# Two sets of constant factors in a graph network kernel: both loaded ahead, constant rows counted in pairs of sets

## What is computed

```python
def layer(h, params):
    W, b, g, beta = params
    h = h * norm_out
    agg = jax.ops.segment_sum(h[src], dst, num_segments=n)
    agg = agg * norm_in
    out = agg @ W + b
    out = _layer_norm(out, g, beta)
    out = jax.nn.gelu(out, approximate=False)
    return (out, None)
h, _ = jax.lax.scan(layer, features, (Ws, bs, ln_g, ln_b))
x = _layernorm(x + h)
```

## Time and profile before

| | |
|---|---|
| median of 3 runs | 1358.86 (1360.18, 1358.86, 1354.14) |
| the profiled execution | 1357.35, its span 1355.7 |
| granted clock, mean of the span | 0.835 |
| busy, share of the span | TensorE 70%, DVE 62%, POOL 56%, ACT 35% |

### The profile page before, as it was taken

How to read it: one execution, slowest core, us unless ns; L and a number is a source line. 1 busy time by engine, 2 the same in 40 slices (tenths; PEclk the granted TensorE clock), 3 DMA queues, 4 the chain that set the end, 5 groups by cost and what they waited for, 6 DMA issues and landing times.

```text
span 1355.7 us, 27832 instructions
## 1 busy us (share of the span) xinstructions
PE 944.8 (70%) x5568; PEld 729.4 (54%) x5568; DVE 841.6 (62%) x1938; ACT 475.7 (35%) x779; POOL 764.9 (56%) x921
## 2 busy tenths in 40 slices
PE   7899857733896978787796898689847889940000
PEld 7675213303785757576674776577736777730000
DVE  9787788835475565747456367346814446757786
ACT  4431232012433333343333433343334433323455
POOL 3477208520565555555654655556536746648885
PEclk9889866755997979899898899699959999975555
DMA  7932499021626354452633632652256679557998
GB/s 273 377 98 60 126 340 383 4 79 36 169 81 202 118 180 125 142 186 106 197 121 131 210 114 97 217 177 87 93 199 191 199 191 396 207 180 252 318 314 300
DMA packets 118241, 246.59 MB, mean 182 GB/s; under 512 B 20271, under 2 KB 21119, under 8 KB 118171
## 3 DMA queue, kind: packets, MB, share of 16 engines
q1 hardware_dynamic: 73868, 133.26, 27.7%
q0 software_dynamic: 31680, 89.43, 22.9%
q10 hardware_dynamic: 12624, 23.14, 4.6%
HBM read 130.14 MB, written 115.64 MB: 181 GB/s over the span
## 4 chain that ended last, share of the span: by engine, by line
PE 37%; DMA 18%; issue 14%; DVE 11%; POOL 11%; DVEq 4%; ACT 3%; ACTq 1%; POOLq 1%; SPq 0%
PE ps_y L1870 6%; DMA rows<-h_rows,slot 6%; PE ps_y L1865 5%; PE ps_y L1866 5%; PE ps_a L1836 5%; DMA h_rows<-rows 5%; POOL rows L752 4%; POOL rows L826 4%; PE ps_y L1710 3%; DMA rows<-h_rows,idx 3%; DVEq L443 2%; DMA constant_factors<-row_factors 2%; PE ps_a L1690 2%; PE ps_z L1729 2%; DVE agg_t L943 1%
## 5 line engine op out<-in xcount | busy, mean ns | idle before, releaser
L1836 PE MATMUL ps_a<-sel,rows 128*128 128x128 f32 x2080 | 302.6, 299 | 93.8 <-DVE sel L1203 53.2
L1836 PEld LDWEIGHTS ps_a<-sel,rows 128*128 128x128 f32 x2080 | 272.0, 207 | 128.5 <-issue 126.8
L1203 DVE TENSOR_SCALAR sel<-iota,by_tile 128x128 f32<-128x128 f32 x307 | 125.2, 411 | 253.0 <-issue 225.4
L752 POOL DMA_INDIRECT rows<-h_rows,slot x230 | 220.1, 957 | 109.6 <-issue 78.6
L1557 ACT ACTIVATE agg_t<-ps_a 128x508 f32 x260 | 155.0, 596 | 216.3 <-PE ps_a L1836 173.8
L777 POOL TENSOR_TENSOR s_lo<-agg_t,s_hi 128x512 fp32r<-128x512 f32 x122 | 157.3, 1292 | 108.5 <-ACT s_hi L1562 108.0
L1865 PE MATMUL ps_y<-w_all,s_hi 128*128 128x512 f32 x488 | 191.6, 393 | 3.5 <-ACT s_hi L1562 2.5
L1866 PE MATMUL ps_y<-w_all,s_hi 128*128 128x512 f32 x488 | 190.2, 390 | 0.0
L1870 PE MATMUL ps_y<-w_all,s_lo 128*128 128x512 f32 x488 | 131.2, 391 | 1.9 <-POOL s_lo L777 1.9
L1358 DVE BATCH_NORM_STATS2 small<-ps_y 128x6 f32<-128x512 f32 x122 | 85.1, 697 | 43.4 <-PE ps_y L1870 43.2
L1562 ACT ACTIVATE s_hi<-agg_t 128x512 fp32r (+1 forms) x122 | 75.9, 628 | 90.7 <-PE ps_y L1870 48.0
(11 more groups left out here) (318 smaller groups left out, 1503.7 us busy)
## 6 DMA issues: line engine op xcount, KB each, us to landing
h_rows<-agg_t SPq DMA_DIRECT2D x2, 22528.0 KB, 67.9
h_rows<-rows SPq DMA_DIRECT2D x92, 256.0 KB, 2.0
h_rows<-rows ACTq DMA_DIRECT2D x87, 256.0 KB, 3.7
out<-agg_t SPq DMA_DIRECT2D x78, 256.0 KB, 4.3
agg_t<-in_x SPq DMA_DIRECT2D x19, 1024.0 KB, 13.5
rows<-in_Ws SPq DMA_DIRECT2D x32, 256.0 KB, 2.7
w_raw<-in_Ws SPq DMA_DIRECT2D x28, 256.0 KB, 4.3
rows<-h_rows,slot POOLq DMA_INDIRECT x230, 3.7
```

Source lines behind the costliest of these rows:

```text
L752: g.indirect_dma_start(out=rows[:, k, :], out_offset=None, in_=table[:, :], in_offset=bass.IndirectOffsetOnAxis(ap=slot[:, k:k + 1], axis=0))\
L1203: return v.tensor_scalar(sel[:, k % GS, :], iota[:, :], rel[:, bass.ds(i, 1)], wgt[:, bass.ds(i, 1)], ALU.is_equal, ALU.mult)
L1836: m = mm(ps_a[k % GS][:, b, :], rows[:, k, b * P:(b + 1) * P], sel[:, k % GS, :], start=True, stop=True)
```

## The change

Factors and vectors get two sets: set 0 on partitions 0 to 9, set 1 on partitions 32 to 41 of the same tiles, each with its own semaphore. Both are loaded at the start of the product stage. The rows of a layer are counted in **duos** of two trios (768 rows, rounded up, at least one); every turn of a loop makes one trio from each set. POOL's loop runs over all duos, and each turn loads both sets for the next one, in the last turn too, where the factors are loaded and not used; the factor table gets 768 more rows in front, so that such a load stays inside it. DVE waits, before its third selection, for all loads of both sets to have landed, in place of the last matmul. The constants `landed` and the semaphore targets follow. Not shown: the table's fills in SP's part (longer by 768 rows), the new counts in POOL's arithmetic (`DUO * P` for `TRIO * P`), and the renamed arguments.

```diff
-ITS_MIN, PAIRS_MIN, TRIOS_MIN = 1, 3, 2
+DUO = 2 * TRIO
+AHEAD_ROWS = DUO * P
+ITS_MIN, PAIRS_MIN, DUOS_MIN = 1, 3, 1
...
-    coef_d = nc.dram_tensor("row_factors", (KINDS, LC, SLACK + PADDED), f32).ap()
+    coef_d = nc.dram_tensor("row_factors", (KINDS, LC, AHEAD_ROWS + SLACK + PADDED), f32).ap()
...
-        co_out, co_vec, co_fac = rows[:, 6:9, :], co_vec_t[0:2 * KINDS, :], co_fac_t[0:2 * KINDS, :, :]
+        co_out = rows[:, 6:9, :]
+        co_vec = [co_vec_t[h * 32:h * 32 + 2 * KINDS, :] for h in range(2)]
+        co_fac = [co_fac_t[h * 32:h * 32 + 2 * KINDS, :, :] for h in range(2)]
...
-        co_in = sem("constant_factors_in")
+        co_in = [sem(f"constant_factors_in{h}") for h in range(2)]
...
-            trios = within(word >> 16, 0, N // (TRIO * P) + 1 - TRIOS_MIN) + TRIOS_MIN if L > 0 else 0
+            duos = within(word >> 16, 0, N // (DUO * P) + 1 - DUOS_MIN) + DUOS_MIN if L > 0 else 0
...
+        def factor_row(rb, g):
+
+            return within(rb - (g + 1) * (TRIO * P) + AHEAD_ROWS, 0, AHEAD_ROWS + SLACK + PADDED - TRIO * P)
...
-            def load_factors(L, n):
+            def load_factors(L, n, h):
 
-                own = coef_d[:, L - 1, bass.ds(trio_row(rb, n), TRIO * P)]
-                g.dma_start(co_fac.rearrange("r a n -> r (a n)"), both(own)).then_inc(co_in, 16)
+                own = coef_d[:, L - 1, bass.ds(factor_row(rb, n * 2 + h), TRIO * P)]
+                g.dma_start(co_fac[h].rearrange("r a n -> r (a n)"), both(own)).then_inc(co_in[h], 16)
...
-                    with pool.Fori(1, constants[0]) as n:
-                        pool.wait_ge(co_pe, (constants[1] + n) * TRIO)
-                        pool.sem_inc(tick, 1)
-                        load_factors(L, n)
+                    with pool.Fori(0, constants[0]) as n:
+                        for h in range(2):
+                            pool.wait_ge(co_pe, (constants[1] + n) * DUO + (h + 1) * TRIO)
+                            pool.sem_inc(tick, 1)
+                            load_factors(L, n + 1, h)
                     stored(pb * 2)
-                    landed = constants[0] + constants[1]
+                    landed = (constants[0] + constants[1]) * 2
...
-                    g.dma_start(co_vec, vec_d[L + 1, :, :].bitcast(f32r)).then_inc(co_in, 16)
-                    load_factors(L + 1, 0)
+                    for h in range(2):
+                        g.dma_start(co_vec[h], vec_d[L + 1, :, :].bitcast(f32r)).then_inc(co_in[h], 16)
+                        load_factors(L + 1, 0, h)
                 w_stage(pairs, pb)
...
-                    trios, cb = constants
-                    dve.wait_ge(co_pe, (cb + trios) * TRIO)
-                    dve.sem_inc(dve_tick, 1)
+                    duos, cb = constants
+                    for h in range(2):
+                        dve.wait_ge(co_in[h], (cb + duos) * 16 + L * 32)
+                        dve.sem_inc(dve_tick, 1)
                 select(tile + AHEAD - 1, AHEAD - 1).then_inc(sel_ok, 1)
...
-                with act.Fori(0, trios) as g:
-                    constant_trio(L, cb + g, g)
+                with act.Fori(0, duos) as g:
+                    for h in range(2):
+                        constant_trio(L, (cb + g) * 2 + h, g * 2 + h)
...
-                with pe.Fori(0, trios) as g:
-                    pe.wait_ge(co_in, (cb + g) * 16 + (L + 1) * 16)
-                    pe.sem_inc(pe_tick, 1)
-                    for k in range(TRIO):
-                        pe.wait_ge(co_h, done((cb + g) * TRIO - TRIO + k + 1))
-                        pe.sem_inc(pe_tick, 1)
-                        mm(ps_co[k], co_fac[:, k, :], co_vec, start=True, stop=True).then_inc(co_pe, 1)
+                with pe.Fori(0, duos) as g:
+                    for h in range(2):
+                        n = (cb + g) * DUO + h * TRIO
+                        pe.wait_ge(co_in[h], (cb + g) * 16 + L * 32)
+                        pe.sem_inc(pe_tick, 1)
+                        for k in range(TRIO):
+                            pe.wait_ge(co_h, done(n - TRIO + k + 1))
+                            pe.sem_inc(pe_tick, 1)
+                            mm(ps_co[k], co_fac[h][:, k, :], co_vec[h], start=True, stop=True).then_inc(co_pe, 1)
```

More of the change, by code:

```diff
@@ L427, in layer_counts @@
             its = within((word >> 8) & 255, 0, NE // UN - ITS_MIN) + ITS_MIN
-            trios = within(word >> 16, 0, N // (TRIO * P) + 1 - TRIOS_MIN) + TRIOS_MIN if L > 0 else 0
+            duos = within(word >> 16, 0, N // (DUO * P) + 1 - DUOS_MIN) + DUOS_MIN if L > 0 else 0
             if earlier is None:
-                return pairs, its, trios, 0, 0, 0
-            return (pairs, its, trios) + tuple(earlier[n] + earlier[n + 3] for n in range(3))
+                return pairs, its, duos, 0, 0, 0
+            return (pairs, its, duos) + tuple(earlier[n] + earlier[n + 3] for n in range(3))
         def place(eng, n, most):
@@ L524, in _ @@
                 sp.wait_ge(made_ok, 2)
-                sp.dma_start(coef_d[n:n + 2, :, SLACK:].rearrange("k l (p n) -> p (k l) n", n=NR),
+                sp.dma_start(coef_d[n:n + 2, :, AHEAD_ROWS + SLACK:].rearrange("k l (p n) -> p (k l) n", n=NR),
                              halves.bitcast(f32).rearrange("p k l n -> p (k l) n")).then_inc(fac_st, 16)
@@ L707, in _ @@
             link(g.memset(num_f[:, 2, 0:1], 0.0))
-            for n, size, extra in ((0, 2 * P, 1), (1, UN * ET, 0), (2, TRIO * P, 0)):
+            for n, size, extra in ((0, 2 * P, 1), (1, UN * ET, 0), (2, DUO * P, 0)):
                 scaled(num_f[:, n, :], num_f[:, n, :], extra * size - (size - 1) / 2 + (1 - extra) * (size - 1), size)
             whole(num_f)
-            for n, least in enumerate((PAIRS_MIN, ITS_MIN, TRIOS_MIN)):
+            for n, least in enumerate((PAIRS_MIN, ITS_MIN, DUOS_MIN)):
                 link(g.tensor_scalar(num_f[:, n, :], num_f[:, n, :], float(least), float(-least), ALU.max, ALU.add))
@@ L806, in _ @@
             for L in range(LAYERS):
-                pairs, its, trios, pb, ib, cb = counts
-                sum_stage(L, hbufs[(L - 1) % 2] if L > 0 else x, its, ib, pb, (trios, cb))
+                pairs, its, duos, pb, ib, cb = counts
+                sum_stage(L, hbufs[(L - 1) % 2] if L > 0 else x, its, ib, pb, (duos, cb))
                 if L + 1 < LAYERS:
@@ L1340, in sum_stage @@
                     bias()
-                    trios, cb = constants
-                    dve.wait_ge(co_pe, (cb + trios) * TRIO)
-                    dve.sem_inc(dve_tick, 1)
+                    duos, cb = constants
+                    for h in range(2):
+                        dve.wait_ge(co_in[h], (cb + duos) * 16 + L * 32)
+                        dve.sem_inc(dve_tick, 1)
                 select(tile + AHEAD - 1, AHEAD - 1).then_inc(sel_ok, 1)
                 if L > 0:
-                    dve.wait_ge(co_h, done((cb + trios) * TRIO))
+                    dve.wait_ge(co_h, done((cb + duos) * DUO))
                     dve.sem_inc(dve_tick, 1)
@@ L1395, in _ @@
             for L in range(LAYERS):
-                pairs, its, trios, pb, ib, cb = counts
-                sum_stage(L, its, pb, ib, pairs * 2, (trios, cb))
+                pairs, its, duos, pb, ib, cb = counts
+                sum_stage(L, its, pb, ib, pairs * 2, (duos, cb))
                 if L + 1 < LAYERS:
@@ L1538, in constant_trio, with constant_stage @@
                 store(TRIO - 1)
-            def constant_stage(L, trios, cb):
-                with act.Fori(0, trios) as g:
-                    constant_trio(L, cb + g, g)
+            def constant_stage(L, duos, cb):
+                with act.Fori(0, duos) as g:
+                    for h in range(2):
+                        constant_trio(L, (cb + g) * 2 + h, g * 2 + h)
             def sum_stage(L, its, pb, ib):
@@ L1592, in _ @@
             for L in range(LAYERS):
-                pairs, its, trios, pb, ib, cb = counts
+                pairs, its, duos, pb, ib, cb = counts
                 if L > 0:
-                    constant_stage(L, trios, cb)
+                    constant_stage(L, duos, cb)
                 sum_stage(L, its, pb, ib)
@@ L1874, in _ @@
             for L in range(LAYERS):
-                pairs, its, trios, pb, ib, cb = counts
+                pairs, its, duos, pb, ib, cb = counts
                 if L > 0:
-                    constant_stage(L, pb, trios, cb)
+                    constant_stage(L, pb, duos, cb)
                 sum_stage(L, its, ib)
```

9 lines of the change are left out of this document (5 added, 4 removed).

## The result

The changed kernel is **slower**, clear of the noise: 1389.22 median of 4 runs (1384.39 to 1394.03) against 1357.66 for the kernel before (1354.14 to 1360.18), a ratio of 1.0229 with a 95% interval from 1.0195 to 1.0262 (so about 2%, and a full 2% is not quite sure). I had forecast 1371 with a range up to 1381. The sign was right, the size was not: 31.6 were lost and I had 13.8 in the sum. The granted clock is 0.833 in the mean of the span, 0.835 before.

What follows compares the result with a forecast made beforehand. The chain that ended last passes through product matmuls, gathers and stores, with constant-factor loads only 2%; ACT's constant work ends the constant stage, gathers right behind. Sum: 1357.35 + 9.9 + 4 x 0 + 2 x 2.5 - 1.1 = 1371.2; range 1354 to 1381.

Steps and rivals of the forecast that it cites:

- Second pair, +9.9: Product stage's start: POOL issues a second pair of loads ahead of the low half, 1.41 in each of seven stages.
- Layers 1 to 4, four times 0: Constant stage, two trios: gathers start 2.3 later behind unread loads, yet the first eviction stays put; 0 per layer.
- a tile 1.55, the step to ACT 0.1: Layer 2, constant stage's end: durations added after the gather's 4.42 to its first matmul, giving eviction at 502.4 against 502.39.
- more than 1 as a sign of being wrong: Layers 1 to 4: the prediction is wrong if the first eviction moves by more than 1.
- the 2.1 that I gave it: Layer 2, constant stage: without the wait for factors, ACT alone could evict the first tile at 500.2, 2.1 earlier.
- Layers 5 to 7, +3.9: Constant stage, trio counts rounded up to even: 2.5 later in each of layers 5 and 6, -1.1 in layer 7.
- DVE's wait, nothing: Before DVE's third selection: its new wait for unread loads to land is hidden by the gather by 2.0, no cost.
- The gathers' delay counts in full: Rival, chance 0.10: the sum stage runs at POOL's pace from its first gather, 17.0 in place of 3.9, time 1384.3.
- ACT alone decides: Rival, chance 0.18: gathers' later start is absorbed, the constant stage gains 13.0, the product stage loses 9.9, time 1354.3.
- the second pair is hidden: Rival, chance 0.06: the product stage's second pair of loads costs nothing, the change then costs 3.9, time 1361.3.
- The twelve waits are the price: Rival, chance 0.04: TensorE's 59.8 of waits for factors go, three trios of 1.8 and 9.9 come, time 1312.9.

Runs made afterwards that it cites:

- experiments 3 and 4: Changed kernel with the second pair issued behind the first two low halves: 1381.95. Kernel before plus an unread second pair at the product stage's start: 1367.84.
- experiment 1: Changed kernel without the loads that nobody uses, DVE waiting for the last matmul as before: 1376.05, ratio 1.0120 to the kernel before.
- Experiment 2: Kernel of experiment 1 with the unread loads back on POOL's queue, into memory that no selection waits for: 1387.73, ratio 1.0233 to the kernel before.
- (6): Kernel of experiment 1 with the kernel before's numbers of trios written in, in place of counts rounded up to even: 1358.21, ratio 0.9997 to the kernel before.
- experiment 7: Two sets, no unread loads, trio counts written in, both pairs moved behind the first two low halves: 1346.82, again 1346.16; its one-set partner 1349.18.

## Why the prediction failed

**The sign held, and the second pair was right; what failed is the slack that was to swallow the gathers' delay in the constant stage.** Point by point:

*Second pair, +9.9.* Right, a little high: 8.1 in the trace, 7.3 and 9.5 in experiments 3 and 4. I priced the second pair as the first; it took 1.14 instead of 1.41.

*Layers 1 to 4, four times 0: the step that failed.* I had the first gather 2.3 later in each: it came 3.8, 2.8, 1.4 and 1.4 later, 9.4 in sum for 9.2, right in the sum and not by layer. (That the gather comes 1.45 behind a load is a misreading of layer 2, where the last store of the product stage landed at 492.55, just as the load's issue ended; experiment 1 has what the gather followed.) That ACT's constant work ends the stage in the kernel before was right too, though the bracket of the first eviction in the earlier trace rows, `[2.78 <-PE ps_a L1836]`, seems to say that ACT waited for the tile. A bracket names the last releaser that the profile knows; where that one was long done, something else held the engine. Two rows of the kernel before, layer 2 (timeline, the first from a window that ends with the first tile):

```profile
498.42 2.05 PE L1836 MATMUL ps_a<-sel,rows 128*128 128x128 f32 x8 [0.44 <-DMA rows<-h_rows,slot]
...
499.32 1.08 ACTq L1530 DMA_DIRECT2D h_rows<-rows  x2
```

The first tile was done at 498.42 + 2.05 = 500.47, and the eviction came 1.92 later, at 502.39. Where the tile ends the wait, as in layer 2 of the changed kernel, it comes 0.38 behind. ACT had issued its last store by 500.40, 1.99 before the eviction. In none of the seven layers of the eleven traces is the eviction less than 1.69 behind that store, not even where the tile had been done for 5.9 (experiment 1, layer 5, shown further below). So it was ACT's own queue that held the eviction back; what ACT does in that time the profile doesn't show.

What failed comes next in the prediction: "a tile 1.55, the step to ACT 0.1: evicted at 502.4. Against 502.39 now, layer 2 gains nothing". For this the gather's way must have had 2.3 to spare in each layer of the kernel before. By the 0.38 it had 1.5 in layer 2, and 0.6, 1.6 and 0.9 in layers 1, 3 and 4. The 1.55 was the mean of four tiles that ran at two levels of TensorE's clock. Windows of that stretch (the clock is the third number from the end):

```profile
498.42:502.70 4.28, 4.28 (x20) 4.27 (x20) 1.31 (x3) 0.99 (x3) 2.50 (x3) 0.50 0.85 267
503.10:504.60 1.50, 1.50 (x13) 1.26 (x11) 0.69 (x3) 0.60 (x1) 0.94 (x1) 1.00 0.92 352
```

The first tile ran at the lower level, 1.2 GHz, and took 2.05, in the changed kernel as well. So of the 10.0 by which the first tiles of the four layers were done later, 4.3 were hidden by ACT and 5.7 reached the first evictions: they came 3.4, 1.0, 0.1 and 1.2 later, counted from the layer's first constant matmul, where I had named more than 1 as a sign of being wrong. Nor did ACT win the 2.1 that I gave it: its last store ended 0.6 to 0.9 earlier. In layer 2 the second trio's second activation waited for a store of the first trio (501.91 in the rows of the constant stage).

The other 2.9 of the 8.6 came behind the first eviction, 2.6 of them in layer 3. There the granted clock over 16 from the first tile was 0.88 before and 0.74 after:

```profile
574.20:590.20 16.00, 13.44 (x88) 12.03 (x88) 5.10 (x21) 6.54 (x11) 10.73 (x12) 0.88 0.74 231
```

and in the changed kernel:

```profile
582.80:598.80 16.00, 14.26 (x86) 13.45 (x87) 4.53 (x18) 5.97 (x10) 9.73 (x11) 0.74 0.62 192
```

That the clock made these 2.6 is likely and not shown: in layer 4 it was 0.71 and 0.81, and nothing was gained there. Over the four layers it was the same, 0.81 and 0.80.

*Layers 5 to 7, +3.9.* The same step, and a trio too cheap. The stages grew by 4.1, 4.4 and 2.2, the first gathers came 4.9, 5.4 and 1.2 later, the first evictions 4.3, 4.7 and 1.2. I had counted on 1.3 to 1.4 to spare in the gather's way; there were 0.5, 0.6 and 0.1. Layer 5 of the changed kernel's timeline, against the earlier trace rows:

```profile
749.21 0.36 ACTq L1542 DMA_DIRECT2D h_rows<-rows  x1
...
755.14 0.34 ACTq L1542 DMA_DIRECT2D h_rows<-rows  x1
...
758.10 1.09 ACT L1547 ACTIVATE rows<-ps_y 128x512 f32<-128x512 f32 x2 [1.73 <-PE ps_a L1840]
...
759.07 0.34 ACTq L1542 DMA_DIRECT2D h_rows<-rows  x1
...
761.38 0.60 ACT L1547 ACTIVATE rows<-ps_y 128x512 f32<-128x512 f32 x1 [1.08 <-PE ps_a L1840]
...
762.13 0.56 POOL L768 DMA_DIRECT2D constant_factors<-row_factors  x1 [3.24 <-PE ps_a L1840]
...
763.97 1.10 POOL L761 DMA_INDIRECT rows<-h_rows,slot  x1 [1.28 <-issue]
764.79 0.35 DVE L1214 TENSOR_SCALAR sel<-iota,by_tile 128x128 f32<-128x128 f32 x1 [8.37 <-DMA constant_factors<-row_factors]
...
768.05 3.33 PE L1851 MATMUL ps_a<-sel,rows 128*128 128x128 f32 x14 [6.85 <-DMA rows<-h_rows,slot]
```

The first store of a trio follows that of the trio before by 5.93 and then 3.93, where I had 4.93 and 3.73. The gather stands behind the fourth trio's matmuls and the unread load. ACT's last store had ended 6.0 before the first eviction, so here the gather's way alone set it.

*DVE's wait, nothing.* Right. It is there (8.37 in the row at 764.79), and the selections that follow it still come before the first tile is on TensorE (764.79 for 768.05 in layer 5, 503.63 for 505.59 in layer 2). Experiment 2 took the wait away and the time stayed.

*The rivals.* "The gathers' delay counts in full" came nearest: I gave it 0.10, +17.0 and 1384.3; the stages grew by 19.3 and the profiled execution took 1384.39. That the two times agree is in part luck: the gathers came 20.8 later in the seven layers, the first evictions 16.0, and the median is 4.8 above this execution, the shortest of four. "ACT alone decides" and "the second pair is hidden" fell with the points above, but once the gathers are early ACT does decide in layers 5 to 7 (experiment 1). "The twelve waits are the price" is refuted: 49 of the 59.8 went, and the kernel became longer; with the unread loads gone too, layers 1 to 4 took what they had taken before (165.8 for 166.4). The Trainium skill's advice to issue early and wait late ("DMA: Bandwidth & Descriptors", section on rules for kernel authors) was followed by the change. These runs show what it leaves open here: the early issue stood on the queue that the next stage's critical issues needed, and the wait that it removed was covered by another, POOL's for the product stage's stores (experiment 1).

**The sum as it stands**, in medians from 1389.2 down: the unread loads 13.2 (experiment 1), then the exact counts 17.8 (6). In the traces, whose spans are 20.2 apart, 15.3 of this lie in layers 5 to 7, which is the rounding, and 4.8 in the product stages, which the written-out loops give. That reaches the kernel before, 1358.2. The second pair, about 8, is still in it; what balances it are those 4.8 and the 5.2 by which layers 5 to 7 are shorter there than in the kernel before (245.8 for 251.0).

## What to carry to other kernels

Idle time in front of an instruction is a price only if nothing else ends the stage. A delay hides only in slack that was there before: measure it layer by layer, from the end of the earlier path's last instruction to the row that waits (here 500.47 to 502.39, less the 0.38 of a step), and not by a mean duration that mixes two levels of the clock. A bracket's releaser that was done long before the row, beyond the usual step, is not what held it. An issue that was added ahead of critical work cost its whole time at once (1.14 a stage), while one that was taken away gave only the way to the next limit (0.5, not 1.39). A loop that loads ahead should not load in its last turn, when what it delays is the first thing the next stage needs.

## What was not expected

*Stores land later while gathers are on their way.* In experiment 1, layer 5, gathers begin at 744.53, while trios are still being made. The fourth trio's activations then waited for the third trio's stores, as its timeline shows (the matmuls from a window that ends with the first tile):

```profile
748.07 0.60 ACT L1547 ACTIVATE rows<-ps_y 128x512 f32<-128x512 f32 x1 [1.73 <-PE ps_a L1840]
...
753.84 2.04 PE L1851 MATMUL ps_a<-sel,rows 128*128 128x128 f32 x8 [1.45 <-DVE sel L1215]
...
755.13 0.60 ACT L1547 ACTIVATE rows<-ps_y 128x512 f32<-128x512 f32 x1 [3.64 <-DMA h_rows<-rows]
757.43 0.60 ACT L1547 ACTIVATE rows<-ps_y 128x512 f32<-128x512 f32 x1 [1.71 <-DMA h_rows<-rows]
...
758.76 1.00 ACTq L1542 DMA_DIRECT2D h_rows<-rows  x2
760.67 0.95 POOL L761 DMA_INDIRECT rows<-h_rows,slot  x1 [8.11 <-DMA h_rows<-rows]
...
761.81 0.59 ACT L1570 ACTIVATE agg_t<-ps_a 128x508 f32 x1 [2.75 <-issue]
```

From the first activation of the third trio to that of the fourth it took 755.13 - 748.07 = 7.1; in the changed kernel, where no gather was on its way, 761.38 - 758.10 = 3.3. The first store of the third trio took 4.8 from issue to landing here and 2.1 there; in layer 6 4.5 and 2.1. The first tile was done at 753.84 + 2.04 = 755.88, and yet it was evicted at 761.81, 2.05 behind the end of ACT's last store (758.76 + 1.00). The seventh gather waited 8.11 for the last trio's stores. This is why layers 5 to 7 gained nothing from earlier gathers (261.1 for 261.7): what the queue gave, the fourth trio took. What slows a store while gathers are in flight is not shown, and no run took the gathers away from these stores alone.

*One kernel's executions differ by what the clock does in a layer.* The two-set kernel of experiment 7 took 175.8 in layers 1 to 4 in its first profiled execution and 169.1 in the second. In layer 4 the granted clock from 650 to 667 was 0.70 in the first (window):

```profile
650.00:667.00 17.00, 13.16 (x79) 12.42 (x78) 6.20 (x22) 5.96 (x10) 7.90 (x9) 0.70 0.53 169
```

and 0.92 in the second:

```profile
650.00:667.00 17.00, 14.01 (x100) 12.60 (x99) 7.17 (x28) 7.19 (x13) 9.48 (x10) 0.92 0.67 197
```

In the first, TensorE had also waited in that layer for a selection that stood behind the layer's bias, which came late to DVE (timeline):

```profile
652.72 0.42 DVE L1356 CAST b_rows<-w_raw 2x512 fp32r<-2x512 f32 x1 [3.68 <-DMA w_raw<-in_bs]
...
654.47 8.33 PE L1861 MATMUL ps_a<-sel,rows 128*128 128x128 f32 x48 [2.42 <-DVE sel L1227]
```

A single trace is therefore good for a stage's mechanism and for sums over several layers, and not for 2 in one layer.
